# Cross attention's row maxima taken one head at a time, in a post-norm decoder layer on one Trainium2 core

## The reference, cut to what matters

```python
scores = jnp.einsum('bqhd,bkhd->bhqk', q * SCALE, k)      # 112 x 375 for each entry and head
attn = jax.nn.softmax(scores, axis=-1)
out = jnp.einsum('bhqk,bkhd->bqhd', attn, v).reshape(B, SQ, INNER)
```

## Time and profile before

| | us |
|---|---|
| median of 3 runs (680.78 to 680.88) | 680.86 |
| the profiled execution's own time | 681.03 |
| its span, first to last instruction | 679.2 |
| VectorE busy in the span | 475.1 |
| TensorE busy in the span | 563.4 |
| ScalarE busy in the span | 406.7 |
| GpSimd busy in the span | 258.6 |

### The profile page before, as it was taken

How to read it: one execution, slowest core, us unless ns; L and a number is a source line. 1 busy time by engine, 2 the same in 40 slices (tenths; PEclk the granted TensorE clock), 3 DMA queues, 4 the chain that set the end, 5 groups by cost and what they waited for, 6 DMA issues and landing times. The chain is left out here.

```text
span 679.2 us, 14737 instructions
## 1 busy us (share of the span) xinstructions
PE 563.4 (83%) x4972; PEld 390.2 (57%) x4972; DVE 475.1 (70%) x921; ACT 406.7 (60%) x979; POOL 258.6 (38%) x292
## 2 busy tenths in 40 slices
PE   5733868899899899999899999899679788899980
PEld 4622545667567567667566666565564564566650
DVE  2895447888888888888888888787658758543333
ACT  2485338677587587587587587565446638544431
POOL 3322024453453453354354354344315612323322
PEclk9775589999999999999999999999857979999995
DMA  8925111211210201200200210401236694333324
GB/s 249 282 50 169 35 64 32 62 46 33 68 39 31 72 33 31 74 31 31 74 31 31 74 31 31 138 32 63 94 103 217 212 323 122 57 56 61 51 32 116
DMA packets 55330, 57.36 MB, mean 84 GB/s; under 512 B 17286, under 2 KB 44238, under 8 KB 55054
## 3 DMA queue, kind: packets, MB, share of 16 engines
q1 hardware_dynamic: 50910, 50.89, 25.0%
q0 software_dynamic: 4384, 5.99, 5.2%
HBM read 46.74 MB, written 10.13 MB: 84 GB/s over the span
## 5 line engine op out<-in xcount | busy, mean ns | idle before, releaser
L734 POOL TENSOR_TENSOR c_rcp<-c_sum,neg_one 112x2 f32<-112x2 f32 x64 | 44.6, 696 | 187.9 <-ACT probs L876 187.9
L738 POOL TENSOR_TENSOR probs<-probs,c_rcp 112x750 f32<-112x750 f32 x64 | 91.8, 1434 | 5.0
L876 ACT ACTIVATE probs<-ps_s,c_neg 112x375 f32<-112x375 f32 x128 | 72.6, 577 | 27.2 <-DVE c_neg L1113 27.1
L769 ACT ACTIVATE kt_hi<-ps_o 128x376 fp32r<-128x376 f32 x64 | 31.8, 497 | 60.2 <-PE ps_o L159 60.2
L1794 POOL DMA_INDIRECT moe_sum<-gsh_hi,xs_in x21 | 33.5, 1595 | 83.3 <-ACT gsh_hi L1842 67.7
L1117 DVE SCALAR_TENSOR_TENSOR cpt_lo<-ps_t,cpt_hi 125x672 f16<-125x672 f32 x64 | 54.3, 848 | 12.0 <-ACT cpt_hi L883 12.0
L1113 DVE TENSOR_REDUCE c_neg<-ps_s 112x2 f32<-112x750 f32 x64 | 59.4, 928 | 1.4 <-PE ps_s L159 1.4
L2071 PE MATMUL ps_h<-w_ex,xst_hi 128*128 (+1 forms) x168 | 58.0, 387 | 2.5 <-DVE xst_lo L1881 2.4
L1482 PE MATMUL ps_t<-ident,probs 112*128 112x112 f32 x384 | 49.2, 265 | 6.8 <-DVE cpt_lo L1117 6.3
L1482 PEld LDWEIGHTS ps_t<-ident,probs 112*128 112x128 f32 x384 | 41.0, 143 | 16.7 <-issue 9.1
L157 PE MATMUL ps_o<-ctxt_hi,w_k_lo 128*128 128x376 f16 x128 | 42.3, 330 | 8.5 <-DVE oct_lo L1126 7.4
(11 more groups left out here) (337 smaller groups left out, 1734.8 us busy)
## 6 DMA issues: line engine op xcount, KB each, us to landing
chunk<-in_L_ffn_ew_dram SPq DMA_DIRECT2D x24, 512.0 KB, 3.5
spare<-in_L_ffn_ew_dram SPq DMA_DIRECT2D x18, 512.0 KB, 5.8
store<-in_L_ffn_ew_dram SPq DMA_DIRECT2D x6, 512.0 KB, 5.2
ctx_raw<-in_ctx_dram SPq DMA_DIRECT2D x8, 375.0 KB
moe_in<-chunk SPq DMA_DIRECT2D x1, 2709.0 KB, 14.2
plain_raw<-in_L_xattn_w_kv_dram SPq DMA_DIRECT2D x2, 1024.0 KB, 15.5
xs_in<-moe_in SPq DMA_DIRECT2D x15, 129.0 KB, 2.1
ctx_all<-in_ctx_dram SPq DMA_DIRECT2D x1, 1800.0 KB, 22.3
```

Source lines behind the costliest of these rows:

```text
L734: pool.tensor_tensor(c_rcp[:, s % 2, :], c_sum[:, s % 2, :], neg_one[:, :], ALU.pow).then_inc(sg["c_rcp_ready"], 1)
L738: pool.tensor_tensor(p, p, r, ALU.mult).then_inc(sg["p_normed"], 1)
L876: act.activation(probs[:, s % 2, h, 0:SK], ps_s[0:N, h, 0:SK], ACT.Exp, bias=c_neg[:, s % 2, h:h + 1], accum_out=c_sum[:, s % 2, h:h + 1]) ...
```

## The change

The one reduction over both heads of a pair (two rows of 375 scores, two maxima) becomes two, one for each head, and each of them signals the semaphore. The exponential of head h waits for 2 (8b + s) + h + 1 signals, just ahead of it, where both waited for the pair's one signal ahead of the first; the wait for the transposes of an earlier pair (`t_full`) now stands ahead of the waits for the maxima.

```diff
             def exps(b, s):
-                act.wait_ge(sg["c_neg_ready"], PAIRS * b + s + 1)
-
                 if later(PAIRS * b + s - 1):
                     act.wait_ge(sg["t_full"], PAIRS * b + s - 1)
                 for h in range(2):
+                    act.wait_ge(sg["c_neg_ready"], 2 * (PAIRS * b + s) + h + 1)
                     act.activation(probs[:, s % 2, h, 0:SK], ps_s[0:N, h, 0:SK], ACT.Exp, bias=c_neg[:, s % 2, h:h + 1],
                                    accum_out=c_sum[:, s % 2, h:h + 1]).then_inc(sg["c_exp"], 1)

             def maxima(b, s):
                 dve.wait_ge(sg["s_full"], PAIRS * b + s + 1)
-                dve.tensor_reduce(c_neg[:, s % 2, :], ps_s[0:N, :, 0:SK], X, ALU.max, negate=True).then_inc(sg["c_neg_ready"], 1)
+                for h in range(2):
+                    dve.tensor_reduce(c_neg[:, s % 2, h:h + 1], ps_s[0:N, h, 0:SK], X, ALU.max, negate=True)\
+                        .then_inc(sg["c_neg_ready"], 1)
```

## The result

The changed kernel takes 694.11 us (median of four runs, 689.37 to 695.5), the one before, run beside it, 680.87 (four runs, 680.78 to 683.05). The ratio is 1.0187, with 1.013 to 1.0243 as its interval. The forecast was 680.8, in a range up to 682.2. The change makes the kernel 13 us slower, by something that is in none of the three rivals. Of all runs in this document one (699.74 us, of the kernel with step 3 alone) fell into a slower state of the chip, and is left out of the medians and ratios.

The account below looks back on a forecast made before the run. No engine is full; waits between TensorE, VectorE and ScalarE in seven nearly equal turns set the time. Step 6's gain and the added reductions' cost sum to -2.03 + 31d = -0.02 us: 680.8 us, range 679.4 to 682.2.

Parts of the forecast that it names:

- three rivals: Faster (678.1 us, chance 0.09), slower (683.4 us, chance 0.09), and no effect (680.9 us, counted with the forecast's 0.82).
- d: VectorE time per added reduction: taken as 0.065 us, bounds 0 and 0.148.
- slower rival: Second reduction waits for the first one's write, d = 0.148 in steps 0, 3, 4: +2.6 us, 683.4 us; chance 0.09.
- Steps 3, 4 and 0: Places where TensorE waits for VectorE's longer way: +d each, seven times in steps 3 and 4, six in step 0.
- Step 6: Seven times, maxima to "Q0": 0.22 us sooner (0.29 - d), limited by TensorE's pv; -1.57 us in all.
- faster rival: Step 6 gains ScalarE's full 0.39 us in seven turns, added reductions hide behind waits: -2.7 us, 678.1 us; chance 0.09.
- the sum: Step 6, steps 3 and 4, step 0 and entry 7 together: -2.03 + 31d, or -0.02 us at d = 0.065.
- The step that failed: Earlier exponentials gain only where what follows sets the end; GpSimd's products and step 3 were given no effect from them.
- The clock: TensorE's granted clock, read in the profile before as the full 2.4 GHz (1.00) in entries 6 and 7.

Follow-up runs that it names:

- step 3 alone: Kernel before, with reductions and waits split per head only in the eight pairs of step 3: 691.3 us, ratio 1.0149.
- the run with the wait for the pair: Changed kernel with two reductions in every step, but both exponentials wait for the second one: 682.54 us, ratio 1.0013.
- the hold alone: Kernel before, no reduction split; GpSimd's multiply of step 6 waits until xnt_lo is done: 678.07 us, ratio 0.9959.
- the hold with the split: Kernel before with reductions split in step 6 only, and GpSimd's multiply there waiting for xnt_lo: 676.21 us, ratio 0.9916.
- the product held: Changed kernel, with GpSimd's multiply in step 3 of entries 0 to 6 waiting until o_self is written: 680.76 us, ratio 0.9992.
- step 3 as it was: Changed kernel, but step 3 keeps its one reduction and one wait: 679.56 us, ratio 0.9974.
- TensorE fed: Changed kernel plus ten unused identity transposes on TensorE ahead of "O1" in step 3 of entries 1 to 6: 684.94 us, ratio 1.0054.
- the kernel before made to collide: Kernel before, no reduction split; x2_norm moved from the end of step 2 to behind step 3's maxima: 692.58 us, ratio 1.0169.

## Why the prediction was wrong

**The cost of a reduction: right.** d was taken as 0.065 us. A reduction of 375 columns lasts 538 ns, as worked out, and the run with the wait for the pair gives 4d = 0.25 us an entry. The slower rival had d = 0.148: it falls, since that would be 0.6 an entry there. The Trainium skill's rule that was weighed for it ("VectorE: DVE Perf Modes", The DRAIN you can't avoid) is not what this pair of reductions does: the second starts 0.46 us after the first (137.51 and 137.97 in entry 0 after), whose record lasts 0.54. The same section says that an instruction which is not held starts earlier.

**Steps 3, 4 and 0, +d each: right where nothing collides.** From the start of the maxima to the start of cpt_lo it is 0.06 to 0.07 us more in each of these steps. That TensorE waits for it is what the 4d of the run with the wait for the pair shows.

**Step 6, -0.29 + d: right in sign, too small, and by another path.** From the maxima to "Q0" it was 4.77 us and is 4.44 in entry 0 and 4.38 in entries 1 to 6: a gain of 0.33 and 0.39, and not 0.22. Entry 0 shows by what. First before:

```profile
137.31 0.93 DVE L1113 TENSOR_REDUCE c_neg<-ps_s 112x2 f32<-112x750 f32 x1
...
140.35 1.43 POOL L738 TENSOR_TENSOR probs<-probs,c_rcp 112x750 f32<-112x750 f32 x1
141.09 0.93 DVE L1092 TENSOR_TENSOR xnt_lo<-xnt_f,xnt_hi 128x224 f16<-128x224 f32 x1 [0.47 <-ACT xnt_hi L842]
142.08 0.22 PE L157 MATMUL ps_a<-xnt_hi,w_q_lo 128*128 128x112 f16 x1 [0.19 <-DVE xnt_lo L1092]
```

and after (the second of the two reductions first; the first starts at 137.51):

```profile
137.97 0.54 DVE L1113 TENSOR_REDUCE c_neg<-ps_s 112x1 f32<-112x375 f32 x1
138.14 0.57 ACT L875 ACTIVATE probs<-ps_s,c_neg 112x375 f32<-112x375 f32 x1 [0.79 <-DVE c_neg L1113]
138.42 0.41 DVE L1012 TENSOR_SCALAR xn<-x,mv,rstd 112x256 f32<-112x256 f32 x1
...
140.21 1.44 POOL L738 TENSOR_TENSOR probs<-probs,c_rcp 112x750 f32<-112x750 f32 x1
141.25 0.64 DVE L1091 TENSOR_TENSOR xnt_lo<-xnt_f,xnt_hi 128x224 f16<-128x224 f32 x1 [0.47 <-ACT xnt_hi L842]
141.95 0.22 PE L157 MATMUL ps_a<-xnt_hi,w_q_lo 128*128 128x112 f16 x1
```

xn is where it was forecast, 0.91 us behind the first reduction, and so in entries 1 to 6 are the first exponential (0.57; in entry 0 0.63) and oct_hi (2.50 us behind it, for 2.73 before: the 0.22 that I had). But "Q0" does not hang on them. xnt_lo, which I took as an instruction of fixed length, waits for the end of GpSimd's product, and "Q0" follows it. From the start of the maxima the product of entry 0 comes 0.34 us sooner (2.70 for 3.04), xnt_lo starts only 0.04 sooner (3.74 for 3.78), and "Q0" gains 0.33. In entries 1 to 6 the product comes 0.39 us sooner, and "Q0" by the same 0.39. The median of xnt_lo goes from 936 to 785 ns:

```profile
L1091 DVE TENSOR_TENSOR xnt_lo<-xnt_f,xnt_hi x8: 393/785/796, 95.8 to 455.9; 128x224 f16<-128x224 f32 x8
```

The full 0.39 us is what the faster rival had, for ScalarE; here it is GpSimd that passes it on. The path that I had worked out does set "Q0" where the product is held: from the hold alone to the hold with the split, it starts 4.33 and 4.10 us after the maxima, 0.23 apart. With the measured gains the sum would have been -0.33 - 6 x 0.39 + 24 x 0.065 = -1.1 us, and that agrees with the kernels without the collision in step 3: ratios of 0.9992 (0.9976 to 1.0009) with the product held, and 0.9974 (0.9953 to 0.9994) with step 3 as it was.

**The step that failed** is this one: "GpSimd's products are read by TensorE a step later, with time in hand", and, for step 3, "VectorE never waits for what ScalarE does after them". Both sentences are true; the product has time in hand and VectorE waits for no semaphore of it. But they follow the earlier exponentials only to those who wait for their result. They leave out when the engine that they release, GpSimd, now uses what it shares with VectorE. Its product starts ahead of o_self, where it had been 0.17 us behind; o_self, on a path that I had named as bound (the last pt_lo, for which TensorE idles), takes 1 us more. That term was missing: six times 0.86 us, 5.2 in all. (With TensorE fed, 5.2 - 1.1 = 4.1 us should be left, and 3.7 are, by the ratio of 1.0054.)

**The clock** was taken as 1.00 throughout, as before. After a gap of 1.33 to 1.35 us TensorE is granted 1.2 GHz for 3.4 or 6.8 us in five of six entries, 10.7 us in sum. That is two thirds of what is lost (10.7 of 5.2 + 10.7), and it hangs on the other third: with the gap filled, it is gone.

The trace of before had two signs. The maximum and minimum of xnt_lo, 394 to 940 ns for one shape, can't be its own work; a mean for the group does not show it. And the starts of the product and of o_self, 171.23 and 171.06, leave 0.17 us, less than the 0.39 that I had ScalarE come sooner.

**The rival that was missing** should have read: the product starts up to 0.39 us earlier in step 3, and o_self up to 2d later, so that the order turns; o_self waits for its end; it decides from 0.17 us on, and costs a microsecond in each of six or seven turns.

**Open.** Why entry 3 after, and entries 4 to 6 of the kernel before made to collide and of the one with step 3 alone, keep their clock after such a gap (1.34, 1.47 and 1.40 us). Their o_self waits as in the others. The kernel fed through the gap shows that the gap is needed for the drop; what decides among equal gaps is not settled here.

## What to carry to other kernels

When an edit makes something earlier, follow every engine that it releases, not only to who waits for the result but to what that engine runs at the same time as others: an order of starts that was 0.17 us from turning was worth 13 us. Look at minimum, median and maximum of VectorE's instructions that have two inputs in SBUF beside a GpSimd instruction that reads SBUF; two values for one shape were the sign of a collision here, and a wait on GpSimd, for work with time in hand, takes it away (0.4% here, on top of 0.45% from the split where it helps). Make a change of order only in the step whose next reader is late.

## What the runs showed of the hardware

- VectorE's 128-column tensor_tensor with both inputs in SBUF lasts 0.29 us alone and 1.29, 1.36 or 1.43 when it starts 0.29, 0.22 or 0.16 us behind a GpSimd product of 1.44 us: it ends 0.14 or 0.15 us after the product, wherever it starts. With 224 columns (xnt_lo) it is 0.39 alone, and it ends 0.24 to 0.25 after the product. The product's own time does not move (1.43 to 1.44).
- The other way round the product pays almost nothing: 0.16 us or more behind o_self it keeps its 1.43 to 1.44 us, though o_self's record lasts 0.29, and 0.12 us behind it takes 1.47 (three kernels, once in each).
- An idle gap of 1.33 to 1.35 us on TensorE, in work that is otherwise at 2.4 GHz, was followed by 3.4 to 6.8 us at 1.2 GHz in five of six entries (after gaps of 1.40 and of 1.47 us in two other kernels, in three of six), a cost of 1.4 to 3.2 us each, more than the gap itself. The low stretches began 0.04 to 1.7 us after TensorE was at work again (in entry 1 at 175.8, after 174.08). With ten transposes in the gap there was none.
